# Second attention of a graph and expert kernel: each of a search's eight gathers waits for an event of its own

## The chip, the cores and the metric

The kernel runs on one core of a Trainium2 chip. The metric is the device time of one execution in microseconds, taken without the profiler; the median of three runs is given. The profiled execution is a separate one and is longer.

## What is computed

The reference passes x (128 graphs x 128 nodes x 128 features, f32) through four blocks, each with a layer norm ahead and a residual sum behind:

```python
x = x + _L0_gnn_ref(_layernorm(x), adj, ...)    # attention inside each graph, masked by adj
x = x + _L0_ffn_ref(_layernorm(x), ...)         # 8 experts with a capacity, one per token
x = x + _L1_gnn_ref(_layernorm(x), adj, ...)    # second attention inside each graph
x = x + _L1_ffn_ref(_layernorm(x), ..., edges)  # attention over 524288 random edges picks 2 of 4 experts
```

The last block needs, for every node, where its edges begin in the list of edges sorted by target:

```python
e = leaky_relu(a_src[src] + a_dst[dst])
ee = exp(e - segment_max(e, dst)[dst])
agg = segment_sum(h[src] * (ee / segment_sum(ee, dst)[dst])[:, :, None], dst)
```

## The kernel before

The 16384 nodes lie in SBUF as 128 partitions (nodes of a graph) by 128 graphs; four graphs are a group, and there are 32 groups. The program has a front part (both attentions, the first experts, and a sort of the edges that is spread through them on VectorE) and, behind a barrier of all engines, a part over the edges with the last experts.

**The second attention** (`att1`, an object of the class Attention) is a software pipeline of steps n = -4 to 32 on ScalarE, TensorE and VectorE. In step n each engine works on several groups: group n is near its end and groups n+2, n+3 and n+4 are at earlier stages. The engines pass the work on by semaphores that count groups: `normed` (ScalarE has normalised a group), `turned` (TensorE transposed it), `featT`, `scored` (TensorE made the scores), `low` (ScalarE scaled them), `exped` (ScalarE took the exponentials), `probs_turned` (TensorE), `probsT` (ScalarE copied the transposed weights out of PSUM, L177), `righted` (TensorE, L264; VectorE adds the bias behind it, L296). Alongside, and for 12 steps behind, runs `gat`, a projection of the result: its steps end in VectorE's copy L389. Its last eleven steps run with no attention left.

**The searches** find where each node's edges begin. GpSimd gathers, by indirect DMA (L1158), 64 sorted keys for each of 128 partitions into a buffer; eight such gathers are a search, there are 32 searches (256 gathers), and the buffer `fetched` holds four searches (FETCHED = 4). VectorE compares (L818) and counts (L821) at the end of a step n >= 0 with n % 4 != 3, so that searches 0 to 24 stand in the attention's steps 0 to 32; searches 25, 26 and 27 stand in the projection's steps 23, 27 and 31, and 28 to 31 behind it. Search k is thus in step k // 3 * 4 + k % 3 as far as search 24.

What sets the order on GpSimd: its instructions run one behind another. Ahead of the eight gathers of search k it waits until search k - 4 has been counted (`looked`), and then issues all eight. No other gather waits. The searches' result, `found`, is written by VectorE behind the last count, and then comes the barrier.

Of the kernel before, what the change touches and what calls it, by code (L numbers as in the profile page):

```python
# [17 lines left out]
GROUPS = GRAPHS // PER  # L18
# [51 lines left out]
def ge(engine, semaphore, value):  # L70

    if isinstance(value, int) and value <= 0:
        return
    engine.wait_ge(semaphore, value)
# [317 lines left out]
def front(nc, sem, a, x, x_in, stats, scratch, rstd, shift, masked, tab, W, fills, ident, ones, upto, row_id, wanted, counted, found,  # L392
# [4 lines left out]
    with ExitStack() as ctx:  # L397
# [18 lines left out]
        def view(lo, *shape):  # L416
# [16 lines left out]
        att1 = Attention(sem, 1, x, masked, stats, rstd, shift, ident,  # L433
                         {"key_side": W["key_row1"][:, :], "query_side": W["query_row1"][:, :],
                          "bias": W["bias1"][:, :], "other": W["other1"][:, :], "fill": fills[:, 1, :]},
                         view, att_small, banks, masked_s, key_made)
# [70 lines left out]
        def rank_views():  # L507

            free = from_to["sorted"][1]

            def part_of(lo, *shape):
                names = "abcd"[:len(shape)]
                return free[:, lo:lo + math.prod(shape)].rearrange(f"p ({' '.join(names)}) -> p {' '.join(names)}", **dict(zip(names, shape)))

            hot_node = free[:, 0:BATCH * P].bitcast(BF16).rearrange("p (u c j) -> p u c j", u=2, c=BATCH)
            hot_graph = free[:, BATCH * P:3 * BATCH * P].bitcast(BF16).rearrange("p (u c j) -> p u c j", u=2, c=BATCH)
            lo = 3 * BATCH * P
            return (hot_node, hot_graph, part_of(lo, 3 * P), part_of(lo + 3 * P, 3 * P).bitcast(I32), part_of(lo + 6 * P, 2, FAN),
                    part_of(lo + 7 * P, 2, FAN).bitcast(I32))
# [26 lines left out]
        def clears(table):  # L546
            return -(-(math.prod(table.shape) // P) // (CLEAR * REPEAT))
# [560 lines left out]
        @block.gpsimd  # L1108
        def _(pool):
            pool.memset(zeros[:, :], 0.0).then_inc(zeroed, 1)  # L1110
            flat = masked[:, :, :].rearrange("p b j -> p (b j)")
            for c in range(GROUPS):
                pool.wait_ge(adj_in[c % ADJ_SLOTS], 16 * (c // ADJ_SLOTS + 1))
                pool.tensor_scalar(flat[:, c * WIDE:(c + 1) * WIDE], adjacent[:, c % ADJ_SLOTS, :], 0, None, ALU.is_le).then_inc(masked_s, 1)
            pool.iota(order_i[:, :], [[-1, EXPERTS]], base=EXPERTS, channel_multiplier=0).then_inc(ordered, 1)
            pool.iota(mark_i[:, :], [[-NODES, GRAPHS]], base=NO_TOKEN, channel_multiplier=-1).then_inc(ordered, 1)
            pool.memset(taken[:, :, :], 0.0).then_inc(ordered, 1)
            pool.wait_ge(part_taken, len(KEY_PARTS))
            pool.memset(resets[:, :, 1:ROWS + 1], 1.0).then_inc(ordered, 1)
            pool.memset(resets[:, :, 0:1], 0.0).then_inc(ordered, 1)  # L1120
            pool.sem_inc(ordered, 1)

            def load(e):
                h = e % 2
                for to, of in ((w1[:, h, :], a["w1"]), (w2[:, h, :, :], a["w2"]), (b1[:, h, :], a["b1T"])):
                    pool.dma_start(to, of[e]).then_inc(w_in[h], 16)
                pool.dma_start(b2[:, h, :], bass.AP(a["b2"].tensor, e * FEAT, [[0, 1], [1, FEAT]])).then_inc(w_in[h], 16)

            pool.wait_ge(slots_clear, clears(slots_dram) * 16)
            for n in range(GROUPS):  # L1130
                if n == GROUPS - GATED:

                    pool.wait_ge(att0.out_s, GROUPS)
                    load(0)
                    load(1)
                pool.wait_ge(sent_normed, n + 1)
                for v in range(PER):
                    q = n * PER + v
                    pool.indirect_dma_start(slots_dram, bass.IndirectOffsetOnAxis(send[:, q:q + 1], 0), sent_feat[:, n % 2, v, :], None,  # L1139
                                            bounds_check=EXPERTS * CAPACITY - 1, oob_is_err=False).then_inc(sent[n % 2], 16)  # L1140
            pool.wait_ge(unwritten, clears(rows_dram) * 16)
            for n in range(STEPS):
                pool.wait_ge(res_s, n + 1)
                pool.wait_ge(token_s, n + 1)
                for r in range(PER):
                    pool.indirect_dma_start(rows_dram, bass.IndirectOffsetOnAxis(token_of[:, n % 4, r:r + 1], 0), res[:, n % 2, r, :], None,  # L1146
                                            bounds_check=TOKENS - 1, oob_is_err=False).then_inc(res_out[n % 2], 16)
                if (n + 1) % SLOT_GROUPS == 0 and n // SLOT_GROUPS + 2 < EXPERTS:
                    load(n // SLOT_GROUPS + 2)
            pool.wait_ge(sorted_s, 1)  # L1150
            pool.iota(rank_views()[3], [[1, 3 * P]], base=0, channel_multiplier=0).then_inc(span_s, 1)
            pool.wait_ge(keys_out, 16)
            pool.wait_ge(ranked_s, 1)
            for n in range(SEARCHES // SEARCH):
                ge(pool, looked, n - FETCHED + 1)
                for c in range(SEARCH):
                    q = n * SEARCH + c
                    pool.indirect_dma_start(fetched[:, n % FETCHED, c, :], None, keys_dram,  # L1158
                                            bass.IndirectOffsetOnAxis(row_ids[:, q:q + 1], 0)).then_inc(fetched_s[n % FETCHED], 16)

# [677 lines left out]
```

## Time and profile before

| | us |
|---|---|
| timed, median of 3 runs | 3117.63 |
| timed, lowest and highest | 3117.0 to 3118.49 |
| profiled execution, its span | 3601.8 |
| of it: up to the first gather of the searches | 1284 |
| second attention with the searches, to 1790 | 506 |
| edges and last experts, from 1790 | 1812 |

The profiled execution is 484 us longer than the timed one. The profile gives each engine's busy time, the idle time ahead of an instruction and what ended it. "remote" as the one that ended a wait means that the semaphore rose long after the end that the profile gives to the instruction which raises it; the ends of TensorE's instructions are modelled. "issue" is time in which the engine waited for nothing that the profile shows. PE is TensorE, PEld its weight loads, DVE VectorE, ACT ScalarE, POOL GpSimd.

### The profile page before, as it was taken

Reading aid. Unit: us, or ns where it says so; the run is one execution under the profiler, and the core shown is the slowest. Engines: PE = TensorE matmul, PEld = TensorE weight load, DVE = VectorE, ACT = ScalarE, POOL = GpSimd, SP = SyncE. Lnnn points to the kernel's source line nnn. Section 1 sums busy time; section 2 is a strip of 40 time slices with the busy share of each in tenths; the row PEclk is TensorE's granted clock in tenths of the full one; section 3 lists DMA queues with packets and bytes.
Section 4 is the critical chain, followed back from the end, with each engine's and each line's share of the span. In section 5 each row is a group of like instructions: output and inputs, shape, how many; then the busy total and the mean of one; then the engine's idle time right before and its main releaser. Section 6 shows DMA issues by size and latency. Waiting matters only on the chain. (4 is left out here: it accounts for less than half of the span.)

```text
span 3601.8 us, 31245 instructions
## 1 busy us (share of the span) xinstructions
PE 1935.1 (54%) x8829; PEld 1316.8 (37%) x8829; DVE 2257.8 (63%) x4422; ACT 1215.1 (34%) x2447; POOL 1857.5 (52%) x1723
## 2 busy tenths in 40 slices
PE   1776642387878645567432455454544444454555
PEld 1555542255655434456311222232222222222223
DVE  8999886989999965554223454454553444544547
ACT  2676754244444323455311122122212122121222
POOL 5400248554544444445575656655655656656561
PEclk9998865699999867777555676676776677767768
DMA  5792001011111121101111111111111111111111
GB/s 198 250 391 84 16 23 39 24 40 37 46 44 41 36 60 40 56 20 23 42 27 23 32 33 32 32 28 38 32 33 32 32 28 31 38 28 32 37 29 30
DMA packets 170130, 192.35 MB, mean 53 GB/s; under 512 B 59241, under 2 KB 126096, under 8 KB 169008
## 3 DMA queue, kind: packets, MB, share of 16 engines
q1 hardware_dynamic: 107616, 118.69, 9.9%
q0 software_dynamic: 57088, 62.48, 8.4%
q10 hardware_dynamic: 5328, 9.97, 0.7%
q8 instruction: 49, 0.80, 0.1%
q14 instruction: 49, 0.40, 0.0%
HBM read 91.70 MB, written 105.25 MB: 55 GB/s over the span
## 5 line engine op out<-in xcount | busy, mean ns | idle before, releaser
L1518 POOL DMA_INDIRECT edge_rows<-node_table,edge_ids x1024 | 1006.5, 983 | 646.2 <-POOLq L1243 345.9
L1646 PE MATMUL x_b_hid<-x_featT,x_w 128*128 128x512 f32 x512 | 362.3, 854 | 281.4 <-PEq L1243 93.5
L1146 POOL DMA_INDIRECT token_results<-arena,token_of x160 | 251.1, 1569 | 294.3 <-ACT arena L1082 216.9
L583 DVE TENSOR_TENSOR sort_ping<-sort_pong 128x1024 f32<-128x1024 f32 (+1 forms) x232 | 395.1, 1744 | 11.3 <-issue 3.8
L1158 POOL DMA_INDIRECT arena<-keys,row_ids x256 | 249.3, 974 | 288.6 <-DVE counts L821 181.0
L583 DVE TENSOR_TENSOR sort_pong<-sort_ping 128x1024 f32<-128x1024 f32 (+1 forms) x230 | 389.9, 1736 | 8.7 <-ACT sort_ping L1016 3.7
L1139 POOL DMA_INDIRECT slots<-arena,send x128 | 177.8, 1389 | 371.9 <-ACT arena L1038 336.9
L1640 PE MATMUL x_b_featT<-ident,x_feat 128*128 128x128 f32 x128 | 34.8, 428 | 581.0 <-issue 385.3
L1653 PEld LDWEIGHTS x_b_res<-x_w,x_hid 128*128 128x128 f32 x2048 | 276.1, 216 | 152.1 <-issue 152.1
L1653 PE MATMUL x_b_res<-x_w,x_hid 128*128 128x128 f32 x2048 | 303.9, 307 | 39.8 <-issue 39.8
L1646 PEld LDWEIGHTS x_b_hid<-x_featT,x_w 128*128 128x128 f32 x512 | 118.9, 262 | 500.2 <-issue 300.9
L1600 ACT ACTIVATE x_hid<-x_b_hid,x_b 128x512 f32<-128x512 f32 x256 | 174.8, 687 | 294.9 <-DMA keys<-sort_pong 129.3
L90 ACT ACTIVATE arena<-x,shift,rstd 128x128 f32<-128x128 f32 x512 | 210.1, 486 | 98.8 <-DMA slots<-arena,send 87.5
L1640 PEld LDWEIGHTS x_b_featT<-ident,x_feat 128*128 128x128 f32 x128 | 22.9, 217 | 587.7 <-issue 587.7
L1607 ACT ACTIVATE w_taken<-w_taken 128x16 f32<-128x16 f32 x32 | 6.9, 216 | 586.5 <-ACTq L1243 357.3
L252 PE MATMUL banks<-arena 128*128 128x129 f32 x512 | 96.4, 347 | 183.3 <-DVE x L279 94.3
L1480 DVE SCALAR_TENSOR_TENSOR x_weighed<-x_b_res,gates,x_weighed 128x128 f32<-128x128 f32 x256 | 72.1, 344 | 193.9 <-DMA adjacent<-in_adj_dram 158.6
L1650 PE MATMUL x_b_res<-x_b,ones 1*128 1x512 f32 x256 | 162.9, 718 | 30.8 <-PEq L1243 27.0
L977 PEld LDWEIGHTS banks<-arena 128*128 128x128 f32 x1280 | 145.9, 192 | 30.3 <-issue 30.3
L252 PEld LDWEIGHTS banks<-arena 128*128 128x128 f32 x512 | 83.9, 248 | 194.1 <-issue 180.0
L977 PE MATMUL banks<-arena 128*128 128x128 f32 x1280 | 153.5, 278 | 0.0
L968 PE MATMUL banks<-arena 128*128 128x512 f32 x320 | 148.5, 608 | 1.8 <-issue 1.8
(346 smaller groups left out, 4059.0 us busy)
## 6 DMA issues: line engine op xcount, KB each, us to landing
edge_table<-zeros SPq DMA_DIRECT2D x8, 5120.0 KB, 35.7
edge_rows<-node_table,edge_ids POOLq DMA_INDIRECT x1024
arena<-slots SPq DMA_DIRECT2D x40, 260.0 KB
slots<-zeros SPq DMA_DIRECT2D x2, 5120.0 KB, 24.4
edge_table<-edge_rows SPq DMA_DIRECT2D x64, 160.0 KB
out_dram<-x_y ACTq DMA_DIRECT2D x33, 256.0 KB
x<-in_x_dram SPq DMA_DIRECT2D x4, 2048.0 KB, 20.2
adjacent<-in_adj_dram SPq DMA_DIRECT2D x32, 256.0 KB, 2.7
```

The source lines that it names most:

```text
L90: last = act.activation(out[:, u, :], x[:, bass.ds(b, 1), :].rearrange("p o f -> p (o f)"), ACT.Identity, bias=shift[:, bass.ds(b, 1)], sc ...
L252: last = pe.matmul(self.b_near[:, v, 0:FEAT + 1], self.probsT[:, v, :], self.right[:, n % self.deep, v, self.near], start=True, stop=True)
L583: step(dve.tensor_tensor(vb[:, :, t, :], va[:, :, 0, :], va[:, :, 1, :], op))
L977: last = pe.matmul(b_res[:, n % 2, r, :], hid[:, n % 2, c, r * P:(r + 1) * P], w2[:, e % 2, c, :], start=False, stop=(r == PER - 1 and c = ...
L1139: pool.indirect_dma_start(slots_dram, bass.IndirectOffsetOnAxis(send[:, q:q + 1], 0), sent_feat[:, n % 2, v, :], None, bounds_check=EXPERT ...
L1146: pool.indirect_dma_start(rows_dram, bass.IndirectOffsetOnAxis(token_of[:, n % 4, r:r + 1], 0), res[:, n % 2, r, :], None, bounds_check=TO ...
L1158: pool.indirect_dma_start(fetched[:, n % FETCHED, c, :], None, keys_dram, bass.IndirectOffsetOnAxis(row_ids[:, q:q + 1], 0)).then_inc(fetc ...
L1518: pool.indirect_dma_start(rows[:, u, c, :], None, table_dram, bass.IndirectOffsetOnAxis(ids[:, u, c:c + 1], 0)).then_inc(rows_in[u], 16)
L1600: act.activation(hid[:, c, :], b_hid[:, c % 2, :], ACT.Gelu, bias=b1[:, c:c + 1]).then_inc(hid_s, 1)
L1646: pe.matmul(b_hid[:, c % 2, :], w1[:, c // HC1, c % HC1 * P:(c % HC1 + 1) * P], featT[:, :], start=True, stop=True).then_inc(hid_mm, 1)
L1650: pe.matmul(b_res[:, e, :, :], ones[0:1, :], b2[0:1, e, :].unsqueeze(1).to_broadcast([1, UNIT, FEAT]), start=True, stop=False)
L1653: last = pe.matmul(b_res[:, e, v, :], hid[:, e * HC1 + c, v * P:(v + 1) * P], w2[:, e * HC1 + c, :], start=False, stop=(v == UNIT - 1 and ...
```

## The change

For search n a step number is worked out, one less than the step in which VectorE looks at it. Gather c of the search then waits for the c-th of eight events of that step: a semaphore of the attention and the group that the step brings to it. Groups past the last are cut to the last (`min(group, GROUPS - 1)`), and a count of zero or less is no wait. The wait for `looked` stays.

```diff
+            def paced_by(c, n):
+
+                return ((att1.probsT_s, n), (att1.low_s, n + 2), (att1.normed, n + 4), (att1.exped, n + 2),
+                        (att1.righted, n + 3), (att1.probs_turned, n + 1), (att1.scored, n + 3), (att1.turned, n + 4))[c]
+
             for n in range(SEARCHES // SEARCH):
                 ge(pool, looked, n - FETCHED + 1)
+                before_step = n // 3 * 4 + n % 3 - 1
                 for c in range(SEARCH):
                     q = n * SEARCH + c
+                    signal, group = paced_by(c, before_step)
+                    ge(pool, signal, min(group, GROUPS - 1) + 1)
                     pool.indirect_dma_start(fetched[:, n % FETCHED, c, :], None, keys_dram,
```

The order on GpSimd from the last instruction ahead of the searches on, of the kernel before; the name behind "waits" is the semaphore, and x31 stands for 31 gathers in a row without a wait:

```order
L1151 IOTA sort_ping 128x384 [waits sort_sorted]
L1158 DMA arena<-keys,row_ids 128x64 [waits rank_done,sort_keys_out]
L1158 DMA arena<-keys,row_ids 128x64 x31
L1158 DMA arena<-keys,row_ids 128x64 [waits looked]
L1158 DMA arena<-keys,row_ids 128x64 x7
```

The same place of the changed kernel, up to the first gather of the second search:

```order
L1151 IOTA sort_ping 128x384 [waits sort_sorted]
L1167 DMA arena<-keys,row_ids 128x64 [waits rank_done,sort_keys_out]
L1167 DMA arena<-keys,row_ids 128x64 [waits g1_low]
L1167 DMA arena<-keys,row_ids 128x64 [waits g1_normed]
L1167 DMA arena<-keys,row_ids 128x64 [waits g1_exped]
L1167 DMA arena<-keys,row_ids 128x64 [waits g1_righted]
L1167 DMA arena<-keys,row_ids 128x64 [waits g1_probs_turned]
L1167 DMA arena<-keys,row_ids 128x64 [waits g1_scored]
L1167 DMA arena<-keys,row_ids 128x64 [waits g1_turned]
L1167 DMA arena<-keys,row_ids 128x64 [waits g1_probsT]
```

The number and the order of the instructions are the same on every engine; what moved is how many of GpSimd's gathers carry a wait: 28 for `looked` and the first one before, nearly all 256 now. The end of GpSimd's work in the front part, of the changed kernel, where the waits of the last searches all name the last group:

```order
L1167 DMA arena<-keys,row_ids 128x64 [waits g1_probsT,looked]
L1167 DMA arena<-keys,row_ids 128x64 [waits g1_low]
L1167 DMA arena<-keys,row_ids 128x64 [waits g1_normed]
L1167 DMA arena<-keys,row_ids 128x64 [waits g1_exped]
L1167 DMA arena<-keys,row_ids 128x64 [waits g1_righted]
L1167 DMA arena<-keys,row_ids 128x64 [waits g1_probs_turned]
L1167 DMA arena<-keys,row_ids 128x64 [waits g1_scored]
L1167 DMA arena<-keys,row_ids 128x64 [waits g1_turned]
L397 UNCONDITIONAL_BRANCH
```

From search 24 on, the first gather waits until `probsT` has counted all 32 groups.

## Rows read from the trace of the kernel before

**Rows 1.** The page: the span, and two groups of instructions (busy, mean ns | idle ahead).

```profile
span 3601.8 us, 31245 instructions
...
L1518 POOL DMA_INDIRECT edge_rows<-node_table,edge_ids x1024 | 1006.5, 983 | 646.2 <-POOLq L1243 345.9
...
L1158 POOL DMA_INDIRECT arena<-keys,row_ids x256 | 249.3, 974 | 288.6 <-DVE counts L821 181.0
```

**Rows 2.** Busy time by stage; the first line names the columns.

```profile
core 0: us, PE busy (x) PEld busy (x) DVE busy (x) ACT busy (x) POOL busy (x), PEclk, DMA share, GB/s
0.00:1284.00 1284.00, 800.50 (x4368) 604.63 (x4368) 1153.71 (x1278) 618.30 (x1338) 539.50 (x372) 0.85 0.26 89
1284.00:1790.00 506.00, 282.59 (x1504) 248.37 (x1504) 249.09 (x709) 223.16 (x530) 249.25 (x256) 0.70 0.16 40
```

**Rows 3.** Line L1158: duration ns min/median/max, and what its engine waited for.

```profile
L1158 POOL DMA_INDIRECT arena<-keys,row_ids x256: 939/947/2746, 1284.2 to 1784.6; - x128
...
  DVE counts L821: 181.0, 22
  issue: 71.0, 233
```

**Rows 4.** Waits of 1300 to 1780: us in total, times, longest.

```profile
ACT arena L181 <- remote: 52.2, 10, 9.4
DVE arena L296 <- remote: 52.0, 7, 14.8
...
DVE masked L389 <- remote: 41.0, 12, 14.0
```

**Rows 5.** Timeline, end of a run of 16 gathers (start us, duration us).

```profile
1404.92 2.08 PE L264 MATMUL banks<-other,arena 128*128 128x128 f32 x8 [1.58 <-issue]
...
1411.42 0.94 POOL L1158 DMA_INDIRECT arena<-keys,row_ids  x1 [0.30 <-issue]
1414.92 0.69 DVE L296 TENSOR_TENSOR arena<-banks,bias 128x512 f32<-128x512 f32 x1 [10.73 <-remote]
```

**Rows 6.** Timeline, the two steps behind it, with a run of 8.

```profile
1422.58 1.91 PE L264 MATMUL banks<-other,arena 128*128 128x128 f32 x8
...
1424.53 0.69 DVE L296 TENSOR_TENSOR arena<-banks,bias 128x512 f32<-128x512 f32 x1 [2.63 <-PE banks L264]
...
1434.01 0.69 DVE L296 TENSOR_TENSOR arena<-banks,bias 128x512 f32<-128x512 f32 x1 [1.21 <-PE banks L264]
```

**Rows 7.** Timeline, the last attention step: gathers, and L177 of the last group.

```profile
1696.99 0.94 POOL L1158 DMA_INDIRECT arena<-keys,row_ids  x1 [11.36 <-DVE counts L821]
...
1715.75 0.95 POOL L1158 DMA_INDIRECT arena<-keys,row_ids  x1 [0.31 <-issue]
...
1720.94 0.58 ACT L177 ACTIVATE arena<-banks 128x512 f32<-128x512 f32 x1
...
1721.52 0.94 POOL L1158 DMA_INDIRECT arena<-keys,row_ids  x1 [4.82 <-DVE counts L821]
```

**Rows 8.** Timeline, the projection's last steps.

```profile
1732.85 0.26 DVE L389 TENSOR_SCALAR masked<-banks 128x96 f32<-128x96 f32 x1 [2.01 <-remote]
...
1735.16 0.26 DVE L389 TENSOR_SCALAR masked<-banks 128x96 f32<-128x96 f32 x1
...
1762.45 1.63 ACT L90 ACTIVATE arena<-x,shift,rstd 128x128 f32<-128x128 f32 x4
...
1765.78 1.63 ACT L90 ACTIVATE arena<-x,shift,rstd 128x128 f32<-128x128 f32 x4
...
1773.28 0.26 DVE L389 TENSOR_SCALAR masked<-banks 128x96 f32<-128x96 f32 x1 [2.61 <-PE banks L384]
```

**Rows 9.** Timeline, the last search, and the first work behind the barrier.

```profile
1775.12 1.28 POOL L1158 DMA_INDIRECT arena<-keys,row_ids  x1 [3.42 <-DVE counts L821]
...
1784.59 0.95 POOL L1158 DMA_INDIRECT arena<-keys,row_ids  x1 [0.30 <-issue]
1787.08 0.69 DVE L818 TENSOR_TENSOR adjacent<-arena,wanted 128x512 f32<-128x512 f32 x1 [7.89 <-DMA arena<-keys,row_ids]
...
1792.92 0.09 DVE L1257 MEMSET due<- 128x32 f32 x1 [3.97 <-PEq L1684]
```

## The prediction

> **What bounds the kernel now.** I first read the busy times by stage: the change touches the second attention alone, 506 of the 3601.8 us of the profiled execution, and there no engine is busy for more than 56%: GpSimd and VectorE 249 us each, TensorE 283 [rows 1, 2]. So a chain of signals sets the time. Then the line of the gathers: 256 of them, 947 ns each in the median, 0.30 us from one to the next (71.0 / 233), so one every 1.25 us when nothing holds GpSimd; it waited 181 us for VectorE's counts, being up to four searches ahead [rows 3]. All 256 at that pace are 320 us: no bound in itself.
>
> Then the waits of the stage. VectorE waited 52.0 + 41.0 = 93 us, and ScalarE 52.2 in one line, for signals of TensorE that came long after the modelled end ("remote") [rows 4]. The timeline shows when: TensorE's L264 ends at 1407.0, GpSimd issues a run of 16 gathers until 1412.4, and VectorE's L296, which waits for L264, starts at 1414.92 [rows 5]. One step later the same pair is 0.04 us apart, and the step from L296 to L296 takes 9.5 us [rows 6]. The late signals stand in and just behind long runs of gathers. That is what the spreading could remove.
>
> Last the stage's end. The last gather ends at 1785.5, VectorE's search 31 waits for it 7.89 us, and the barrier opens at 1792.9 [rows 9]. Here GpSimd is on the path that sets the end, and TensorE and ScalarE are done.
>
> **The body: steps 0 to 31.** Every wait that is added is on GpSimd; queued behind it are only later gathers, and VectorE is who waits for those. Three searches, 24 gathers, fall to four steps: 24 x 1.25 = 30 us of GpSimd in 4 x 9.5 = 38 us [rows 3, 6]. The first search's fourth gather waits for `exped`, near the end of a step, say 8 us in (my estimate from the 9.5 us step); the 20 gathers behind it then run back to back, since their events lie in the past, and end at 8 + 21 x 1.25 = 34 us. They land 1.5 us later (1785.5 to 1787.08 [rows 9]), at 36. VectorE reads the third search at the end of the third step behind, at 4 x 9.5 = 38 or a little later. So I cost the gathers' later start in the body at nothing: the cover is the 2 us and more between 36 and 38, and it is gone when a step takes under 9 us. Past that the searches wait.
>
> Note that this does not make the runs shorter: 20 to 22 gathers in a row, against 8 or 16 now. What breaks a run is that five of eight events are TensorE's or behind it: a late signal holds the gathers too.
>
> **The tail, the term of the sum.** For search 24 the step number is 31, so its first gather waits for `probsT` of the last group; the waits behind it name the last group too and are then over. L177 of the last group ends at 1720.94 + 0.58 = 1721.5 [rows 7]. From there the changed kernel has eight searches to fetch, 64 x 1.25 = 80 us: the last gather ends at 1801.5. Waits for `looked` don't lengthen this: search 31 needs search 27, counted by 1775.1 [rows 9], when GpSimd still has some 21 gathers to go. The kernel before had fetched searches 24, 25 and 26 by 1716.7 [rows 7] and had 40 gathers left at 1721.5; it ended at 1785.5 [rows 9]. Difference **+16.0 us**: 30 us of gathers more, less 14 us that GpSimd idled for VectorE. What hides a gather in the tail now is the projection, which ends at 1773.5 [rows 8], and that cover is used up.
>
> The price depends on how long the projection takes, as the kernel before follows it and the changed one doesn't. Its steps are 3.33 us apart where nothing is late (1762.45 to 1765.78); ten of them from 1735.16 end at 1768.5, not at 1773.28, and the 2.01 us of late signal ahead goes too [rows 8]: before would end 6.8 us earlier, and the price is +22.8. At the other end, if a gather took only its 0.95 us without the gap, 64 take 60.8, and before needs 53.6 (to 1775.12) + 7.6 = 61.2: price about 0. So 0 to +23; I take **+18**, close to the rows' own pace of 1.25.
>
> **Do the late signals exist in the timed runs?** The timed runs are 484 us shorter than the profiled one. In the edge stage GpSimd's gathers waited 345.9 us for its own queue's waits [rows 1]; even if all that went, 138 us must be saved before it, and the first stage has only 1284 - 1153.7 = 130 us in which VectorE isn't busy [rows 2]. So a good part of the 138 most likely comes from the second attention, whose late signals hold VectorE for 93. I conclude that they are mostly of the profiled execution. Against it: if the gathers' pace is shorter than 1.25 in timed runs, the edge stage alone could give the 484, and I can't exclude that. I cost the gain in the body at 0 and keep 93 as its bound.
>
> The Trainium skill bears on this: its page "SBUF — State Buffer", section "SBUF: two separate sides", says that PE and ACT never wait on anyone at SBUF's ports. By that rule gathers on GpSimd have no way to hold TensorE, the body would give back nothing, and the sum would be the tail alone; the rows of the profiled execution show TensorE's signal 7.9 us late beside such a run [rows 5], and they would give back up to 93 us.
>
> **The sum.** Against the profiled execution's 3601.8: body 0, tail +16. Against the timed median: 3117.6 + 18 = **3136 us**. The timed one gets the larger tail because I take its signals to be on time.
>
> **Rivals.**
> - *The tail, as above*: +7 to +28, 3125 to 3146. Chance 0.45.
> - *Faster: late signals dissolve.* If they are real, pacing stops the 32 gathers in a row at the start, behind which VectorE waited up to 14.8 us [rows 4], and ends a run as soon as TensorE is late. Half of 93 returned less the tail's 16: -30, 3087 us; all of it: -77, 3041. It decides from 16 / 93, a sixth of those waits. For it: every long "remote" wait that I looked at lies beside gathers. Against: the 484 us, and that the new runs are no shorter. Chance 0.33.
> - *No change that can be measured.* The gathers' pace in timed runs is near 0.95, or a small gain in the body meets the tail: 3112 to 3123. Chance 0.15.
> - *Slower still: searches wait in the body.* If undisturbed steps take 8.2 us, the third search's keys land at 36 and are wanted at 33 to 34, so VectorE waits some 2.5 us in each of 8 cycles: +20 on top, 3156. It needs steps under 9 us and a pace of 1.25. Chance 0.07.
>
> **How the numbers follow.** The forecast is the likeliest case, 3136, its own range 3125 to 3146. A difference of 0.2%, 6.2 us, is about what a measurement of this kernel can tell from no change. Slower by more: 0.45 + 0.07 = 0.52; within: 0.15; faster: 0.33. The range goes down into the faster case as far as 3080, which leaves out about 0.12 below, and up to 3147, which leaves out 0.07.
>
> **What the profile of the changed kernel would show.** The tail is right if the last 64 gathers run back to back from the end of the last L177, with the last search starting some 82 us behind it instead of 65.6. The body is right if L818 waits for gathers nowhere but there. The faster rival is right if the "remote" waits of L296 and L389 fall well below 93 us and the timed run follows; if they fall and the timed run doesn't, they belonged to the profiled execution. I am wrong if the gap between the last L177 and the last L818 doesn't grow.

## The result, and the profile of the changed kernel

| | us, median | lowest to highest |
|---|---|---|
| kernel before | 3117.32 | 3115.4 to 3118.49 |
| changed kernel | 3159.53 | 3158.51 to 3164.74 |

The ratio is 1.0142, 95% interval 1.0128 to 1.0156: **slower by 42.2 us**. The forecast was 3136 with a range up to 3147, so the sign was right and the time lies 12.5 us outside the range.

The profiled execution of the changed kernel is as long as its timed ones (3158.1 against 3158.51 to 3164.74), unlike the one of before, which [rows 1] showed at 3601.8. Differences between those two profiles are therefore no measure of the change. The first experiment was the kernel before once more, without an edit; its profiled execution spans 3111.8 us, and it is the "before" of every comparison below.

The page of the changed kernel, the lines that answer to [rows 1] (busy, mean ns | idle ahead, and what ended most of it):

```profile
span 3158.1 us, 31233 instructions
...
L1527 POOL DMA_INDIRECT edge_rows<-node_table,edge_ids x1024 | 996.4, 973 | 313.2 <-issue 297.9
...
L1167 POOL DMA_INDIRECT arena<-keys,row_ids x256 | 250.3, 978 | 192.2 <-issue 69.0
```

The same gathers of the kernel before, in its second profile:

```profile
L1158 POOL DMA_INDIRECT arena<-keys,row_ids x256 | 248.7, 972 | 150.0 <-issue 75.6
```

The 256 gathers are as long as they were (978 and 972 ns); GpSimd's idle time ahead of them is 192.2 - 150.0 = **42.2 us** more. That it equals the difference of the timed medians to the tenth is chance: the spans of these two profiled executions differ by 46.3 us, but nearly all of the loss is here. By stages, as [rows 2], first the changed kernel and then the kernel before:

```profile
core 0: us, PE busy (x) PEld busy (x) DVE busy (x) ACT busy (x) POOL busy (x), PEclk, DMA share, GB/s
0.00:1286.00 1286.00, 799.33 (x4344) 605.75 (x4368) 1154.55 (x1279) 618.36 (x1338) 539.92 (x373) 0.85 0.26 89
1286.00:1699.00 413.00, 248.37 (x1488) 222.00 (x1504) 248.44 (x708) 220.94 (x530) 250.12 (x256) 0.76 0.19 49
1699.00:3158.00 1459.00, 749.85 (x2957) 419.19 (x2957) 852.01 (x2436) 366.34 (x579) 1058.36 (x1095) 0.74 0.19 40
```

```profile
1286.00:1657.00 371.00, 240.41 (x1488) 214.67 (x1504) 248.42 (x713) 219.94 (x530) 249.18 (x258) 0.78 0.22 55
1657.00:3112.00 1455.00, 757.36 (x2957) 423.04 (x2957) 852.39 (x2434) 366.20 (x579) 1054.71 (x1093) 0.74 0.19 40
```

The stage with the searches takes 413 us in place of 371; ahead of it nothing moved, and behind it 4 us did, for which no run gives a cause. The stage that the first profile showed as 506 us [rows 2] is 371 in an execution as long as the timed ones: the stage that I reasoned about was over a third longer than the one that is timed.

What GpSimd waited for at the gathers of the changed kernel, as [rows 3]:

```profile
L1167 POOL DMA_INDIRECT arena<-keys,row_ids x256: 942/947/2501, 1285.8 to 1690.8; - x128
...
  issue: 69.0, 225
  DVEq L802: 36.6, 1
  ACT arena L181: 32.4, 3
  ACT arena L204: 23.2, 7
  ACT arena L177: 18.0, 6
  ACT arena L90: 5.3, 6
  PE banks L237: 4.7, 4
  PE banks L221: 2.4, 2
  PE banks L264: 0.7, 2
...
  DVE adjacent L818: 49.9, 14
```

and the waits of the kernel before in its second profile, over the stage (us in total, times, longest):

```profile
DVE arena L296 <- PE banks L264: 39.0, 30, 5.7
POOL arena L1158 <- DVE counts L821: 37.9, 7, 12.2
...
DVE adjacent L818 <- DMA arena<-keys,row_ids: 14.0, 2, 8.6
```

The 36.6 us stands ahead of the first gather in both and is no part of the change. Without it and without "issue", the gaps of 0.30 us between gathers, the new events held GpSimd for 32.4 + 23.2 + 18.0 + 5.3 + 4.7 + 2.4 + 0.7 = 86.7 us, and the wait for `looked` (the counts of L821) held it for 37.9 before and no longer. VectorE waited for keys 14 times, 49.9 us, where it did twice, 14.0 us. I use this sum of GpSimd's waits as a measure in the experiments: **87** in the changed kernel, **38** in the kernel before.

The end of the stage in the changed kernel, in answer to [rows 9] (start us, duration us, in brackets the idle time ahead):

```profile
1672.99 0.69 DVE L818 TENSOR_TENSOR adjacent<-arena,wanted 128x512 f32<-128x512 f32 x1 [6.78 <-DMA arena<-keys,row_ids]
...
1682.76 0.69 DVE L818 TENSOR_TENSOR adjacent<-arena,wanted 128x512 f32<-128x512 f32 x1 [8.36 <-DMA arena<-keys,row_ids]
...
1690.83 0.96 POOL L1167 DMA_INDIRECT arena<-keys,row_ids  x1 [0.30 <-issue]
1693.29 0.69 DVE L818 TENSOR_TENSOR adjacent<-arena,wanted 128x512 f32<-128x512 f32 x1 [9.12 <-DMA arena<-keys,row_ids]
...
1699.16 0.09 DVE L1266 MEMSET due<- 128x32 f32 x1 [4.00 <-PEq L1693]
```

and in the kernel before:

```profile
1648.28 0.95 POOL L1158 DMA_INDIRECT arena<-keys,row_ids  x1 [0.30 <-issue]
1650.80 0.69 DVE L818 TENSOR_TENSOR adjacent<-arena,wanted 128x512 f32<-128x512 f32 x1 [8.56 <-DMA arena<-keys,row_ids]
...
1656.60 0.09 DVE L1257 MEMSET due<- 128x32 f32 x1 [3.94 <-PEq L1684]
```

In both the last gather is followed 1.5 to 1.6 us later by the last L818 and then by the barrier, which opens 42.6 us later in the changed kernel. The last L177, from which the prediction counted the tail, starts at 1608.97 in the changed kernel and at 1584.2 in the kernel before. So 24.8 of the 42.6 us lie ahead of it and 17.8 behind it, where the prediction had 0 and 18. That is only where the loss lies. Which waits bring it, those of the body (searches 0 to 23) or those of the tail (24 to 31), is what the second and third experiments separate, and they don't give 24.8 and 17.8.

### The profile page after: what moved, and what is told of

It reads as the page before. It is cut to its first block and busy times, and to the rows that moved or that the text cites. A ratio compares the mean times of both kernels' runs of the same rounds, so it can differ in the third digit from the quotient of the medians.

```text
span 3158.1 us, 31233 instructions
## 1 busy us (share of the span) xinstructions
PE 1797.5 (57%) x8789; PEld 1246.9 (39%) x8829; DVE 2255.0 (71%) x4422; ACT 1205.6 (38%) x2447; POOL 1848.4 (59%) x1723
## 5 line engine op out<-in xcount | busy, mean ns | idle before, releaser
L1527 POOL DMA_INDIRECT edge_rows<-node_table,edge_ids x1024 | 996.4, 973 | 313.2 <-issue 297.9
L1167 POOL DMA_INDIRECT arena<-keys,row_ids x256 | 250.3, 978 | 192.2 <-issue 69.0
L1400 DVE TENSOR_TENSOR win_score<-win,masked 128x320 f32<-128x320 f32 x64 | 28.6, 489 | 456.8 <-DMA win<-edge_table,win_ids 455.6
L1655 PE MATMUL x_b_hid<-x_featT,x_w 128*128 128x512 f32 x512 | 310.8, 761 | 28.3 <-PEq L1252 28.3
L1662 PEld LDWEIGHTS x_b_res<-x_w,x_hid 128*128 128x128 f32 x2048 | 247.5, 198 | 97.2 <-issue 97.2
L1662 PE MATMUL x_b_res<-x_w,x_hid 128*128 128x128 f32 x2048 | 272.7, 288 | 0.0
L1655 PEld LDWEIGHTS x_b_hid<-x_featT,x_w 128*128 128x128 f32 x512 | 107.6, 238 | 217.8 <-ACT x_hid L1609 126.4
L252 PE MATMUL banks<-arena 128*128 128x129 f32 x512 | 87.9, 325 | 150.9 <-DVE x L279 92.3
L1659 PE MATMUL x_b_res<-x_b,ones 1*128 1x512 f32 x256 | 143.6, 640 | 27.8 <-PEq L1252 27.8
L977 PEld LDWEIGHTS banks<-arena 128*128 128x128 f32 x1280 | 145.9, 192 | 30.3 <-issue 30.3
```

What stands on the lines that cost most here:

```text
L977: last = pe.matmul(b_res[:, n % 2, r, :], hid[:, n % 2, c, r * P:(r + 1) * P], w2[:, e % 2, c, :], start=False, stop=(r == PER - 1 and c = ...
L1527: pool.indirect_dma_start(rows[:, u, c, :], None, table_dram, bass.IndirectOffsetOnAxis(ids[:, u, c:c + 1], 0)).then_inc(rows_in[u], 16)
L1655: pe.matmul(b_hid[:, c % 2, :], w1[:, c // HC1, c % HC1 * P:(c % HC1 + 1) * P], featT[:, :], start=True, stop=True).then_inc(hid_mm, 1)
L1659: pe.matmul(b_res[:, e, :, :], ones[0:1, :], b2[0:1, e, :].unsqueeze(1).to_broadcast([1, UNIT, FEAT]), start=True, stop=False)
L1662: last = pe.matmul(b_res[:, e, v, :], hid[:, e * HC1 + c, v * P:(v + 1) * P], w2[:, e * HC1 + c, :], start=False, stop=(v == UNIT - 1 and ...
```

## Theories

**G, GpSimd is the bound.** The gathers need 256 x 1.25 = 320 us in a stage of 371; the stage ends just behind the last of them, and so every microsecond that an added wait holds GpSimd, less what it saves at `looked`, is time. Rivals: the **tail** alone (my prediction, with the body free); **S**, each wait that a gather carries costs GpSimd something, whatever it waits for; **E**, the waits inside a search are the cost, not that of its first gather; and the **pause at the start**, about 30 us at the second gather (below), as the whole loss. The expectations of the first runs have G in an earlier form, "theory L": the keys come later, and GpSimd is behind at the end.

The eight kernels ran in two groups of four, and each group had the kernel before timed beside it (3115.82 and 3116.2 us). All ratios are to it.

## Experiments

### The kernel before, once more

No edit. 

> The kernel before, once more, for a second profiled execution. The changed kernel's profile has a span of 3158.1 us against 3159.5 us timed, and no late signal of TensorE, while the kernel before's had 3601.8 against 3117.3 and many. If the late signals belonged to that one execution, the span is now 3112 to 3122 us, the second attention with the searches takes some 370 us (415 of the changed kernel's less 42), and no wait of VectorE there is 'remote'. If they belong to the kernel before, the span is near 3600 again.

Timed 3114.13 us, ratio 0.999 (0.998 to 0.9999), profiled span 3111.8. It is the same kernel, and so 2 or 3 us are not to be told from nothing here. Its waits, shown above, name no late signal: L296 waits for the modelled end of L264, 39.0 us in 30 waits, at most 5.7, where [rows 4] had 52.0 us in 7 waits for "remote", up to 14.8. L296 runs once for each group; these are the ones of groups 4, 20 and 30:

```profile
1335.88 0.69 DVE L296 TENSOR_TENSOR arena<-banks,bias 128x512 f32<-128x512 f32 x1 [2.37 <-PE banks L264]
...
1492.71 0.69 DVE L296 TENSOR_TENSOR arena<-banks,bias 128x512 f32<-128x512 f32 x1 [2.53 <-PE banks L264]
...
1562.61 0.69 DVE L296 TENSOR_TENSOR arena<-banks,bias 128x512 f32<-128x512 f32 x1 [0.28 <-PE banks L264]
```

A step is thus 9.8 us long in the mean of the first 16, from group 4 to 20, and **7.0 us** in the mean of the 10 behind them (from 6.0 to 8.0). In the stretched execution the same two stretches have 13.0 and 12.5 us; the 9.5 of [rows 6] is one of its short steps. VectorE's searches 15 and 21, in the late part:

```profile
1515.78 0.68 DVE L818 TENSOR_TENSOR adjacent<-arena,wanted 128x512 f32<-128x512 f32 x1
...
1570.32 0.68 DVE L818 TENSOR_TENSOR adjacent<-arena,wanted 128x512 f32<-128x512 f32 x1
```

VectorE takes six searches in 54.5 us there, and their 48 gathers need 60. The kernel before lives on its lead there, the gathers that it has made ahead of their use: its last wait for the counts ends at 1487.76, and from then to 1649.2 GpSimd never stops, for 128 gathers.

```profile
1487.76 0.94 POOL L1158 DMA_INDIRECT arena<-keys,row_ids  x1 [8.98 <-DVE counts L821]
```

The late signals belonged to one execution. The gain in the body, the faster rival, has nothing to come from.

### The waits in the body alone

```diff
-                    ge(pool, signal, min(group, GROUPS - 1) + 1)
+                    if n < 24:
+                        ge(pool, signal, min(group, GROUPS - 1) + 1)
```

> The added waits stay on searches 0 to 23 and are gone from 24 on. Theory L (the change only makes keys come later: GpSimd issues its first run 30 us later, VectorE waits for keys in the body, and GpSimd is behind at the end): in the changed kernel search 24's gathers followed search 23's without a pause (1610.1, 1610.4), so nothing is won back: 3152 to 3160 us. My prediction's tail (the cost is the waits of search 24 and later): the cost goes, 3117 to 3130. Theory S (each gather with a wait of its own costs GpSimd more, 42 us / 256 = 0.16 us each): 192 of 256 waits, 3149 us.

3159.86 us, ratio 1.0144 (1.0127 to 1.0161): as slow as the whole change. Searches 24 to 31 carry none of the new waits, and VectorE still waits for keys 50.0 us in 16 waits. The tail alone falls as the explanation of the change. The last L177 and the last gather of this run:

```profile
1610.13 0.60 ACT L177 ACTIVATE arena<-banks 128x512 f32<-128x512 f32 x1 [0.32 <-PE banks L221]
...
1691.08 0.95 POOL L1168 DMA_INDIRECT arena<-keys,row_ids  x1 [0.31 <-issue]
```

From the end of the one to the end of the other it is 81.3 us, against 64.5 in the kernel before and 82.2 in the changed kernel. The loss behind the last L177 is there without any wait in the tail: the waits of the body bring it.

### The waits in the tail alone

```diff
-                    ge(pool, signal, min(group, GROUPS - 1) + 1)
+                    if n >= 24:
+                        ge(pool, signal, min(group, GROUPS - 1) + 1)
```

> The added waits are on searches 24 to 31 alone; the rest is as before. My prediction's tail: GpSimd stands until the last group's probsT and then has 64 gathers, 80 us, to go, with nothing slowed ahead of it: +16 to +23, 3133 to 3141 us. Theory S: 64 waits, +10, 3128 us. If search 24's wait is no cost at all by itself: 3117.

3130.9 us, ratio 1.0051 (1.0034 to 1.0067): +15.1 us. GpSimd's own line, at search 24, and its sum over the stage:

```profile
1582.82 0.94 POOL L1168 DMA_INDIRECT arena<-keys,row_ids  x1 [16.96 <-DVE counts L821]
```

```profile
  DVE counts L821: 52.9, 9
```

(What ended the 16.96 us is put down to L821, which came last by the profile; the wait that is new is the one for L177, whose last instruction starts at 1581.5, ends 0.6 later and is followed by the gather at 1582.82.) The sum of waits goes from 37.9 to 52.9, +15.0, and the time by +15.1 (10.6 to 20.9 by the interval). So the step that I predicted exists, and its size is within the range that I gave it. But the two parts don't add up: 44.0 + 15.1 is 59, and both together are 42.2. Once the body has used up GpSimd's lead, the tail's wait has nothing left to take. In the changed kernel the gathers of search 24 follow those of search 23 without a gap:

```profile
1608.97 0.58 ACT L177 ACTIVATE arena<-banks 128x512 f32<-128x512 f32 x1
...
1610.38 0.95 POOL L1167 DMA_INDIRECT arena<-keys,row_ids  x1 [0.30 <-issue]
```

### All waits kept, four steps earlier

```diff
-                before_step = n // 3 * 4 + n % 3 - 1
+                before_step = n // 3 * 4 + n % 3 - 5
```

> All eight waits stay, each for an event four steps earlier, which is about when the buffer comes free anyway (it holds four searches, three to four steps). The spread over a step's events remains, the lateness goes. Theory L: 3112 to 3122 us, no wait of VectorE for keys in the body. Theory S: all 256 waits stay, 3159 us. If spreading has a worth of its own, below 3112.

3113.82 us, ratio 0.9998 (0.9988 to 1.0007). Nearly every gather still carries its wait, and the time is that of the kernel before. S falls: it asked for 3159 us. A wait that is over when GpSimd comes to it costs nothing that these runs show. The waits of this kernel at the gathers:

```profile
  issue: 70.1, 230
...
  DVE counts L821: 27.7, 6
  ACT arena L90: 5.8, 4
```

With the small ones behind them the sum is 42 us, against 38.

### One step earlier

```diff
-                before_step = n // 3 * 4 + n % 3 - 1
+                before_step = n // 3 * 4 + n % 3 - 2
```

> All eight waits, each for an event one step earlier. Theory G: search 15 starts behind the probsT of step 18, near 1500, search 16 near 1510.5, and no pause from there: 16 searches end near 1671, 22 us behind the kernel before: 3134 to 3142 us. If a step of 6 to 9 us were cover enough, as my prediction's body had it (keys landing 2 us before they are wanted), VectorE would not wait and only a tail cost of some 6 us would be left: 3122 us.

3139.37 us, ratio 1.0076 (1.0057 to 1.0094): +23.2 us. One step more of lead gives back 19 of 42 us. VectorE still waits for keys (36.9 us, 8 waits). GpSimd's sum is 65.8, that is +27.9.

### Only a search's first gather waits

```diff
-                    ge(pool, signal, min(group, GROUPS - 1) + 1)
+                    if c == 0:
+                        ge(pool, signal, min(group, GROUPS - 1) + 1)
```

> Of each search only the first gather waits for its event (probsT), the seven behind it follow at once. The runs so far show that the stage ends when GpSimd ends: from search 15 or 16 on it is never idle in the kernel before, since the steps there take 6.2 us, three searches are wanted every 25 us, and 24 gathers take 30. So what counts is when it gets to search 15 (theory G). Here that waits for the probsT of step 19, 1503.4 in the run with the tail's waits alone, against 1469.1 for search 15 and 1487.8 for search 16 in the second profile of before: 17 searches of 10.05 us from 1503.5 end at 1675, 26 us later than before's 1649: 3138 to 3146 us. If the seven other waits were what costs (theory E), only the tail's wait is left: 3131 us, as with the tail's waits alone.

3149.28 us, ratio 1.0101 (1.0078 to 1.0124): +33.1 us. E falls, since the first gather's wait alone brings three quarters of the loss; but I had put 3138 to 3146, and missed by 3. The line of the gathers:

```profile
  ACT arena L177: 72.0, 12
  DVE counts L821: 3.2, 1
```

75.2 us in 13 waits, +37.3 over before. I had placed the start of search 15 at 1503.4, from the run with the tail's waits alone; it is 1511.14. About half of that is the execution and not the waits: its first gather starts at 1290.06, against 1286.31 in the run with the tail's waits. VectorE's first wait for keys comes later still, at 1522.18. From there on the steps themselves are held up, which I had left out, and with them the events that the next searches wait for: the last L177 starts at 1605.69, against 1584.17 in the kernel before. The other seven waits of a search bring the remaining 9 us.

### The first four searches free

The second gather of the changed kernel waits 29.91 us for ScalarE's scaled scores of a group:

```profile
1316.72 0.96 POOL L1167 DMA_INDIRECT arena<-keys,row_ids  x1 [29.91 <-ACT arena L181]
```

Is that pause the loss? The edit leaves the first 32 gathers as they were.

```diff
-                    ge(pool, signal, min(group, GROUPS - 1) + 1)
+                    if n >= 4:
+                        ge(pool, signal, min(group, GROUPS - 1) + 1)
```

> Searches 0 to 3 are gathered without the added waits, so that GpSimd doesn't stand for 30 us behind its first gather. By the account of idle times those 30 us are most of the 41 that GpSimd loses. Theory G: they would be given back by search 4's waits anyway, since every later search is tied to its step; what remains is the 3 us of VectorE's waits in searches 0 and 2: 3153 to 3160 us. If the pause at the start is the cost by itself: 3129 us.

3154.29 us, ratio 1.0127 (1.0107 to 1.0148): 4 to 5 us less than the whole change, which the intervals don't separate, and not 30. The pause moves to the first gather that waits:

```profile
1357.05 1.10 POOL L1168 DMA_INDIRECT arena<-keys,row_ids  x1 [25.84 <-ACT arena L177]
```

What costs is the distance that the waits keep between gather and search, and not the place of one pause.

### The other way: seven searches held

If idle time of GpSimd is time, then taking the wait for `looked` away should gain. This is the kernel before with three more buffers, in a part of the array `adjacent` that isn't in use there; nothing of the change is in it.

```diff
-        BATCH, SEARCH, FETCHED = 8, 8, 4
+        BATCH, SEARCH, FETCHED = 8, 8, 7
...
-        fetched = view(10256, FETCHED, SEARCH, FAN)
+        in_arena = view(10256, 4, SEARCH, FAN)
+        in_adjacent = flat_adj[:, SEARCH * FAN:4 * SEARCH * FAN].rearrange("p (k c f) -> p k c f", k=3, c=SEARCH)
+
+        def fetched(n):
+            k = n % FETCHED
+            return in_arena[:, k, :, :] if k < 4 else in_adjacent[:, k - 4, :, :]
```

> The kernel before with a buffer for seven searches in place of four (three of them in the tile adjacent, which is free here), so that GpSimd waits less for VectorE's counts: the change turned round. Theory G: GpSimd's 38 us of idle time behind the start go, its last gather ends near 1612, and VectorE sets the end: search 27 at 1631, the last four right behind it, at 1637 in place of 1651: 14 us less than the kernel before, 3099 to 3105 us. If GpSimd is not what bounds the stage: 3116 us.

3100.66 us, ratio 0.9949 (0.9929 to 0.9968): **15.5 us faster than the kernel before**, and the fastest of this study. Two lines of the gathers, their wait, and the stage's end:

```profile
L1164 POOL DMA_INDIRECT arena<-keys,row_ids x160: 940/944/2925, 1290.4 to 1622.5; - x160
L1164 POOL DMA_INDIRECT adjacent<-keys,row_ids x96: 940/944/2755, 1331.7 to 1582.1; - x96
...
  DVE counts L827: 4.0, 1
```

```profile
1622.47 1.35 POOL L1164 DMA_INDIRECT arena<-keys,row_ids  x1 [0.30 <-issue]
...
1638.96 0.69 DVE L824 TENSOR_TENSOR adjacent<-arena,wanted 128x512 f32<-128x512 f32 x1
...
1640.41 0.69 DVE L824 TENSOR_TENSOR adjacent<-arena,wanted 128x512 f32<-128x512 f32 x1
...
1644.37 0.09 DVE L1263 MEMSET due<- 128x32 f32 x1 [2.09 <-PEq L1690]
```

GpSimd waits 4.0 us in place of 37.9 and ends 25 us earlier (1623.8 against 1649.2), but the barrier opens only 12.2 us earlier. (The first gather of this execution starts 3.3 us later than in the kernel before; counted from it, the barrier gains 15.5.) VectorE now ends the stage: its last searches stand 1.45 us apart without a wait. There the gain ends: in this profile VectorE waits for no keys at all, so that a still deeper buffer would have nothing to shorten. I did not build one.

## The sum of GpSimd's waits and the time

The column "all idle time" has the gaps booked to "issue" in it too; the kernel before has 150.0 us there.

| kernel | waits, us | over before | all idle time, over before | time over before, us |
|---|---|---|---|---|
| four steps earlier | 42 | +4 | -1.1 | -2.0 |
| tail alone | 52.9 | +15.0 | +14.4 | +15.1 |
| one step earlier | 65.8 | +27.9 | +22.8 | +23.2 |
| first gather only | 75.2 | +37.3 | +35.7 | +33.1 |
| first four free | 75.7 | +37.8 | +32.5 | +38.1 |
| body alone | 85.4 | +47.5 | +40.4 | +44.0 |
| the change | 86.7 | +48.8 | +42.2 | +42.2 |

The times follow either sum within 7 us. Where a gather's wait ends inside its 0.30 us gap, the profile books the gap to the event, so that "issue" falls (69.0 against 75.6) as the waits rise; that is why the two sums differ. That GpSimd bounds this stage is shown from both sides, by waits added and by a wait taken away. Taken away, only half of its idle time comes back as time (32.1 us less idle, 15.5 us less time), since VectorE is the next bound.

## Why the prediction was wrong

**"All 256 at that pace are 320 us: no bound in itself."** This is the step of the reasoning that failed, and the next one rests on it. I held 320 us against a stage of 506 [rows 2], though I had written myself that the timed runs were 484 us shorter and that much of it likely came from this stage. In an execution as long as the timed ones the stage is 371 us, and GpSimd's gathers with their gaps fill 86% of it. Its busy time, 249 us, leaves the gaps out and so shows 67%. The pace, 1.25 us, was right and is the same in every profile.

**"So I cost the gathers' later start in the body at nothing: the cover is the 2 us and more between 36 and 38."** This is the term of the sum that failed: 0 in the prediction, **+44.0 us** when measured as a change of its own, and that is as much as the whole change costs. Its condition was right, "gone when a step takes under 9 us", but it was held against one step length, the 9.5 us of [rows 6], for the whole body. The undisturbed steps take 9.8 us in the mean as far as group 20, and 7.0 in the ten behind. In searches 0 to 14 VectorE waits only 3.5 us for keys, in searches 15 to 23 it waits 18.1. The working, a gather held to the fourth event of the first search and 20 back to back behind it, holds for search 12 (14.68 us at its fourth gather, for `exped`); in the late part the hold is at the first gather of search 15 (5.17 us), and 23 follow without a pause. VectorE's wait at search 16:

```profile
1529.65 0.69 DVE L818 TENSOR_TENSOR adjacent<-arena,wanted 128x512 f32<-128x512 f32 x1 [3.22 <-DMA arena<-keys,row_ids]
```

**The tail, +16 to +23, taken as +18.** Alone its waits measured +15.1 us, within the term's range of 0 to +23, and there the mechanism is the one predicted. In the changed kernel it is not at work. The first gather of search 24 starts at 1610.38, 0.30 us behind the last one of search 23 and 0.8 us behind the end of the last L177: GpSimd comes too late to be held. Behind that L177 (1609.55) the last gather ends 82.2 us later (1691.79), where it was 64.5. These 17.8 us look like the predicted 18, but the run with the body's waits alone has 16.8 of them, so the likeness is luck. The working had one part wrong for the timed runs as well: the 14 us for which GpSimd idled in the tail [rows 7] belong to the stretched execution; undisturbed, the kernel before has no idle time there, because it had already lost its lead earlier. What I missed is that the term isn't one of its own: it is the same lead, taken away by whichever wait comes first. The band of this case in the list of rivals, +7 to +28, was also wider than the term that it rests on.

**"Do the late signals exist in the timed runs?"** Judged right, by subtraction of times alone: I asked for 138 us ahead of the edge stage, and the second attention is 135 us shorter in the second profile. The late signals are in none of the nine later profiles. The rule of the Trainium skill, page "SBUF — State Buffer", section "SBUF: two separate sides", that PE and ACT never wait on anyone at SBUF's ports, agrees with these: the changed kernel's L296 waits for nothing but the modelled end of L264, 45.7 us in 30 waits. No run tests the ports by themselves, and since the page speaks of ports alone, the prediction's "no way to hold TensorE" went further than the page does. What it would have made of the sum, that the body gives nothing back, is so; what the body takes, it does not speak of. But I drew only half of the conclusion: if the signals go, the steps get shorter as well, and every cover worked out from them goes too. The chances bear this: "faster" had 0.33, though it needed signals that the same text called absent.

**The rivals.** "Searches wait in the body" had 0.07 and gave 3156; it is what happened, and 3159.5 was measured. Its 20 us of VectorE's waits are 21.6 in the profile, though not as 2.5 in each of eight cycles, and the tail's 18 that it added was not a second cost; the nearness is in part luck. Its condition, undisturbed steps of less than 9 us, followed from the accounting that I believed. Faster: its premise is gone. No change: it asked for a pace near 0.95, and the pace is 1.25.

**The signs to look for.** "The last 64 gathers run back to back from the end of the last L177": they do, 82.2 us, as said, but they do so with the body's waits alone too, so the sign doesn't tell the tail's cost from the body's. "L818 waits for gathers nowhere but there": wrong, 21.6 us of its 49.9 are in searches 0 to 23. "If they fall and the timed run doesn't, they belonged to the profiled execution": so it was.

**Open:** why that one execution of the kernel before was stretched by 490 us. No experiment was made on it. The traces say where: up to the first gather of the searches it is no longer than the other (1284 against 1287 us), the second attention is 135 us longer and the stage over the edges 357.

## What to carry to other kernels

Compare the profiled span with the timed one first; if it is much longer, a cover worked out from its steps must be worked out again for the shorter stage, where each engine's fixed work is a larger share. Work it out for the shortest run of steps too, and not for one step read somewhere: here the same loop had a stretch of 9.8 us and one of 7.0. Count an engine's gaps of issue with its work before you say that it is not the bound: 256 x 0.95 us was 67% of the stage, 256 x 1.25 us was 86%. And a wait that ties a prefetch to the step just before its use takes away the lead that lets it be late elsewhere. Four steps ahead, which is about when the buffer came free anyway, the same waits cost nothing.

## What was not expected of the hardware

- The same kernel was profiled at 3601.8 and at 3111.8 us. In the first, VectorE waited up to 14.8 us for a signal of TensorE, and all 52 such waits of VectorE and ScalarE in the second attention end within 4 us of a gather; but gathers with their gaps fill 320 of its 506 us, so that this says little of the cause. In the second there is none, though 128 gathers follow one another without a pause.
- A wait which is already over costs GpSimd nothing that could be measured: with waits on 237 of 256 gathers, nearly all of them over when it came to them, the kernel took the time of the one without them (3113.82 against 3114.13 us), and the gap between gathers stayed at 0.30 us.
